# TensorE given products that nobody reads, in its waits of the prologue, the first chunk, the dt steps, the last sums and the first norm

## What is computed

```python
A = -jnp.exp(A_log)
xp = jnp.einsum('bld,rd->blr', x, x_proj_w)          # dt_in (16), B (16), C (16)
dt = softplus(jnp.einsum('blr,dr->bld', dt_in, dt_proj_w) + dt_proj_b)
dA = jnp.exp(dt[..., None] * A)
dBx = dt[..., None] * B[:, :, None, :] * x[..., None]
# h = dA_t * h + dBx_t along the 1024 tokens; y = sum over n of h * C_t, plus D * x
x = _layernorm(x + mixer(x))
x = _layernorm(x + silu_ffn(x))                      # 512 -> 1792 -> 512, float16 weights
x = _layernorm(x + attention(x))                     # 32 heads of 16, causal
x = _layernorm(x + int4_ffn(x))                      # 512 -> 1376 -> 512
```

## Time and profile before

| what | value |
|---|---|
| median of 3 runs | 903.16 us |
| the three runs | 903.12, 903.16, 908.68 us |
| the profiled execution | 909.25 us |
| its span, first to last instruction | 907.5 us |
| mean granted clock of PE | 0.955 |
| busy in the span: PE, DVE, ACT, POOL | 825.7, 647.1, 439.0, 308.9 us |

### The profile page before, as it was taken

One profiled execution on the slowest core, in us unless ns is written; L12 is line 12 of the kernel. 1 busy time (PEld: TensorE's weight loads), 2 busy tenths in 40 slices (PEclk: granted clock), 3 DMA queues, 4 the chain that ended last, 5 costly groups with the idle time before them and its releaser, 6 DMA issues.

```text
span 907.5 us, 19543 instructions
## 1 busy us (share of the span) xinstructions
PE 825.7 (91%) x8137; PEld 386.2 (43%) x8137; DVE 647.1 (71%) x912; ACT 439.0 (48%) x578; POOL 308.9 (34%) x219
## 2 busy tenths in 40 slices
PE   8758787786999999999979999999987999999997
PEld 2434343444544445455533444334423444444443
DVE  4998989995565334445567999999956978876334
ACT  4975646645754311244434666767676243333100
POOL 0798989993001010254420222121223222231000
PEclk8597979998999999999977999999998999999999
DMA  7800000004230000000000000000022113330011
GB/s 227 332 2 3 3 2 3 3 4 162 93 111 1 1 1 0 1 1 1 1 1 1 2 2 3 2 1 2 2 60 112 57 44 126 113 113 0 0 47 46
DMA packets 21937, 38.25 MB, mean 42 GB/s; under 512 B 6993, under 2 KB 12881, under 8 KB 21858
## 3 DMA queue, kind: packets, MB, share of 16 engines
q1 hardware_dynamic: 21858, 37.11, 11.9%
HBM read 34.87 MB, written 2.16 MB: 41 GB/s over the span
## 4 chain that ended last, share of the span: by engine, by line
PE 70%; DVE 17%; issue 6%; POOL 3%; ACT 2%; SPq 1%; DMA 1%; POOLq 0%; DVEq 0%; ACTq 0%
PE ps L864 13%; PE ps L664 11%; PE ps L641 8%; PE ps L891 6%; DVE arena L1543 6%; PE ps L815 6%; PE ps L715 5%; PE ps L751 5%; DVE arena L1344 4%; POOL arena L1196 3%; PE ps L799 3%; PE ps L514 3%; PE ps L558 2%; PE ps L728 2%; PE ps L755 2%
## 5 line engine op out<-in xcount | busy, mean ns | idle before, releaser
L1543 DVE TENSOR_REDUCE arena<-ps 128x1 f32<-128x512 f32 (+3 forms) x320 | 183.7, 630 | 20.8 <-PE ps L755 14.7
L1134 ACT ACTIVATE arena<-ps 128x1024 f32<-128x1024 f32 (+2 forms) x160 | 144.1, 941 | 77.9 <-PE ps L799 77.7
L1196 POOL TENSOR_TENSOR arena<-arena 128x1024 f32<-128x1024 f32 x64 | 159.7, 2524 | 14.3 <-DVE arena L1344 9.2
L1344 DVE TENSOR_TENSOR_SCAN arena<-arena,ps 128x1024 f32<-128x1024 f32 x64 | 142.6, 2272 | 9.8 <-ACT arena L979 6.0
L864 PE MATMUL ps<-arena 128*128 128x512 f16 x528 | 114.3, 379 | 1.6 <-DVE arena L1433 1.6
L1245 POOL TENSOR_SCALAR_AFFINE_SELECT arena<-arena 128x512 f32<-128x512 f32 x64 | 42.5, 664 | 185.6 <-ACT arena L1134 185.6
L664 PE MATMUL ps<-arena 128*128 128x512 f16 x448 | 97.5, 379 | 1.5 <-DVE arena L1474 1.5
L751 PE MATMUL ps<-arena 64*128 64x512 f16 (+3 forms) x384 | 97.6, 343 | 0.7 <-DVE arena L1543 0.7
L558 PE MATMUL ps<-arena 64*128 64x64 f16 x3072 | 61.5, 197 | 36.5 <-DVE arena L1344 32.7
L979 ACT ACTIVATE arena<-arena,negA 128x1024 f32<-128x1024 f32 x64 | 73.1, 1147 | 43.8 <-DVE arena L1344 42.8
L558 PEld LDWEIGHTS ps<-arena 64*128 64x128 f16 x3072 | 53.6, 100 | 90.4 <-DVE arena L1344 74.6
(11 more groups left out here) (155 smaller groups left out, 982.8 us busy)
## 6 DMA issues: line engine op xcount, KB each, us to landing
arena<-in_w_q_dram SPq DMA_DIRECT2D x11, 768.0 KB, 4.4
arena<-c_rows SPq DMA_DIRECT2D x16, 512.0 KB, 11.0
arena<-in_w_s_dram SPq DMA_DIRECT2D x11, 384.0 KB, 4.5
arena<-in_x_fm_dram SPq DMA_DIRECT2D x8, 256.0 KB, 4.0
out_dram<-arena SPq DMA_DIRECT2D x8, 256.0 KB, 2.0
arena<-in_wg_dram SPq DMA_DIRECT2D x1, 1792.0 KB, 9.7
arena<-in_wu_dram SPq DMA_DIRECT2D x1, 1792.0 KB, 7.3
arena<-in_wd_dram SPq DMA_DIRECT2D x1, 1792.0 KB, 11.3
```

The source lines that it names most:

```text
L1134: nc.scalar.activation(dst, src, ACT.Exp, scale=float(HD) ** -0.5).then_inc(exp_done, 1)
L1196: nc.gpsimd.tensor_tensor(hC[i % 4][:], hst[i % 3][:], c_all[:, n, :], ALU.mult).then_inc(hc_done, 1)
L1344: nc.vector.tensor_tensor_scan(hst[i % 3][:], dA[i % 3][:], banks(2 * (i % 2), 2), 0.0, ALU.mult, ALU.add).then_inc(scan_done, 1)
L1543: nc.vector.reduce_max(maxima_slot(half, k), ps[:, ring_bank(n), 0:len(heads) * w].rearrange("p (a w) -> p a w", a=len(heads)), AX).then_i ...
```

## The change

PE gets 153 more matmuls, each 128 rows by 128 columns of weights and 512 moving columns in float16. They write to bank 5 or bank 7 while nothing there is needed, and nobody reads them. 20 of them multiply the tile of zeros `warm`, the other 133 the gate weights `wg0_sb`, for which PE waits once on `ld_w0` between the two halves of `turn_dtx(0)`. In chunks 1 and 2 PE also waits for `z_pos` of the next chunk before they run, so that bank 5 is free. No other engine's program changes, apart from line numbers.

```diff
+            def idle_products(n, bank, tile=None, cols=HALF):
+
+                for _ in range(n):
+                    if tile is None:
+                        nc.tensor.matmul(banks(bank, 1), warm[:, 0:P], warm[:], start=True, stop=True)
+                    else:
+                        nc.tensor.matmul(banks(bank, 1), tile[:, 0:P], tile[:, 0:cols], start=True, stop=True)
...
-            x_linear(0, range(DC)).then_inc(xp_done, 1)
-            x_linear(1, range(DC // 2))
+            for c in range(DC - 1):
+                x_linear(0, (c,))
+                idle_products(2, 5)
+            x_linear(0, (DC - 1,)).then_inc(xp_done, 1)
+            idle_products(3, 5)
+            for c in range(DC // 2):
+                x_linear(1, (c,))
+                idle_products(2, 5)
             pe.wait_ge(ld_small, 4 * 16)
             dt_first(0)
-            x_linear(1, range(DC // 2, DC)).then_inc(xp_done, 1)
+            x_linear(1, (DC // 2,))
+            idle_products(2, 5)
+            x_linear(1, (DC - 1,)).then_inc(xp_done, 1)
+            idle_products(2, 5)
...
             dt_linear(1)
+            idle_products(3, 5)
             turn_dtx(0, range(TT // 2))
+            pe.wait_ge(ld_w0, 16)
+            idle_products(10, 5, wg0_sb[:, 0, :])
             turn_dtx(0, range(TT // 2, TT))
...
+                    if c == 0:
+                        idle_products({0: 2, 1: 10, 2: 10, 3: 5, 4: 5, 12: 0, 13: 0, 14: 0, 15: 0}.get(n, 4), 5, wg0_sb[:, 0, :])
+                    elif c + 1 < DC and 8 <= n < 11:
+                        pe.wait_ge(z_pos, c + 1)
+                        idle_products(5, 5, wg0_sb[:, 0, :])
             for n in range(NS - LAG, NS):
                 add_y((DC - 1) * NS + n)
+                idle_products(4, 5, wg0_sb[:, 0, :])
...
             for t in range(4):
                 turn_first(t)
+            idle_products(10, 7, wg0_sb[:, 0, :])
             turn_normed(0)
+            idle_products(3, 7, wg0_sb[:, 0, :])
             turn_normed(1)
             turn_first(4)
             turn_normed(2)
             turn_first(5)
             turn_normed(3)
+            idle_products(4, 7, wg0_sb[:, 0, :])
```

## The result

The changed kernel took 908.57 us (median of 22 runs, 903.35 to 914.67). The kernel before, beside it on the same chip, took 904.14 us (22 runs, 899.96 to 910.72). The ratio is 1.0048, with a 95% interval of 1.0031 to 1.0065: 4.4 us slower, a small loss, and well inside the 1% that the prediction called no change. Further down, the ratios of y1 and y3 leave out one disturbed run each (1060.17 and 977.9 us), which their medians keep.

What follows compares the result with a forecast made beforehand. DVE was taken to set the pace in the long low-clock stretch, PE in the prologue and at the beginnings of chunks 1 and 2. 2.6 + 0 + 0 + 0 + 0 - 0.7 = +1.9 us gave 905.0 us, range 899.5 to 910.0.

Steps and rivals of the forecast that it cites:

- main case: Whole kernel: forecast 905.0 us, bracket 902.5 to 907.5, chance 0.50.
- rival B: Around 20 us and early chunk 0: low clock meets the products, slower; 907.8 us, up to 910; chance 0.18.
- Input products: Prologue: fifteen products ahead of the last input product delay `xp_done` and DVE's copy; +2.6 us.
- Turns: Prologue, around the two turns: -0.35 us at full clock, +1 to +2 at low clock; entered as 0.
- Chunk 0: Chunk 0: 60 products hidden by DVE with the clock up, cost 0; low clock up to 2 us per ten.
- Beginnings of chunks: Starts of chunks 1 and 2: no reason for the falls to go; 0 against the median, ends -4.4 and +4.4.
- Dt steps: Chunks 1 and 2: thirty products fit PE's waits; 0, or a gain of 1 to 2 where the clock falls.
- Last sums and norm: Last four sums and first norm: products keep the clock up, turns run faster; -0.7 us, between 0 and -1.5.
- A: Beginnings of chunks 1 and 2: all falls go, clock stays up; 902.5 us, perhaps 900; chance 0.22.
- C: Whole kernel: products, 20 of them on zeros, do not hold the clock, only costs remain; 909.4 us; chance 0.05.
- D: All 51 us of low clock were lost time and half comes off; 886 us; chance 0.02.

Runs made afterwards that it cites:

- y1: Changed kernel without its products ahead of chunk 0 (123 left), PE's wait for `ld_w0` moved behind the turns: 904.37 us, ratio 0.9985.
- y3: Changed kernel without the products of the prologue, the last sums and the norm (90 left, in the chunks): 905.19 us, ratio 1.0005.
- x2: Kernel before with only the 17 products between and behind the input products: 908.57 us, ratio 1.0042.
- x1: Changed kernel without the 17 products between and behind the input products, other 136 kept: 904.39 us, ratio 1.0008.
- x3: Changed kernel with the 15 products between the input products put in one block ahead of the last input product: 909.03 us, ratio 1.0044.
- z4: Changed kernel run again, unchanged, for a second trace: 908.88 us, ratio 1.0040.
- x4: Kernel before run again, unchanged, for a second trace: 903.17 us, ratio 0.9986.
- y4: y1 plus four products behind the last step of chunks 0 to 2 and three in step 0 of chunks 1 and 2: 903.95 us, ratio 0.9982.
- z1: y4 without the three products of step 0; four behind the last step of chunks 0 to 2 stay: 903.91 us, ratio 0.9996.
- z2: z1 with POOL's step 6 product in chunks 1 and 2 waiting until DVE's first dt instruction ends: 900.32 us, ratio 0.9961.
- y2: Kernel before with only the 33 products behind the last four sums and in the first norm: 904.35 us, ratio 0.9991.
- z3: Kernel before with only the POOL wait of z2: 903.22 us, ratio 0.9995.

## Why the prediction was right, and where a term was off

The forecast was 905.0 us, against a median of 903.16 for the kernel before; the change measured +4.4 us, the forecast says +1.9. Direction, place of the loss and the verdict within 1% were right, and 908.57 is inside the range, near its upper end. It is not inside the 902.5 to 907.5 of the main case, which had a chance of 0.50; it lies in the bracket of rival B (907.5 to 910), whose condition the profile after does not meet. About 1 us of the distance is the baseline, 904.14 in the comparison and 903.16 in the forecast. That the range holds the number owes something to luck: some 2 of the 4.4 us are in no term of the sum (see what stays open). Point by point:

**Input products, +2.6 us: right in mechanism, too small.** The copy went from 14.70 to 19.10 in the pair of profiles. Over all traces it starts at 15.2 on average in the ten without these products (14.70 to 15.79) and at 18.5 in the three that interleave them (18.20, 18.31, 19.10), where 17.3 was forecast: 3.4 us. The first scan moves by about 3.0, to 29.75 and 30.56 in the two traces of the changed kernel, where 28.9 was forecast. The term of the sum that was mis-sized is the price of one product: "0.21 us each" was read from sixteen of one shape in a row, and between float32 products it is 0.34. Six groups (the one ahead of `dt_first` makes no new change of shape for an input product) at 0.14 for the slower pair behind them, six pairs of products at 0.54 and one three at 0.76 are 4.8 us; less PE's waits for the second half of x in the profile before, 0.28 us ahead of 9.70 and 0.11 ahead of 10.70 (the lower end of the prediction's 0.4 to 0.8), 4.4. In the other nine traces without these products the first of the two waits alone is 0.6 to 1.8 us, and in the three with them there is none; the products fill that wait, and so the mean over the traces is 3.4 and not 4.4. x2 shows that this term stands alone for the loss, x1 that without it there is none to be measured, x3 that in a block the price is 0.23.

**Turns, taken as 0 between -0.35 and +1 to +2: both ends occur.** With the clock up (after) the wait of DVE before the first scan shrank from 0.59 to 0.30 us. With the clock low (x1) the first scan came at 28.07; the other nine without input products have it at 27.1 on average, so the ten products cost 1 us there. In the changed kernel the input products themselves come ahead of this place, and in its two traces the clock was up for the ten (after) or fell for 3.4 us (z4). In both it is 11.45 us from DVE's copy to the first scan, against 11.9 in the kernel before: the gain of 0.35 came, as about 0.45.

**Chunk 0, 0: right.** It lasts 48.9 or 49.0 us in 13 of the 14 traces, with the 60 products and without them, at the full clock and with 15 us of low clock in it (49.3 in x4, where the clock fell at 64.9). DVE hides PE there in both directions.

**Beginnings of chunks, taken as 0 against the median with 4.4 us either way: right that the change does not steer them, wrong in their worth.** Over the 14 traces a fall stands at the first beginning in 6 and at the second in 5. Of the kernel before, one trace has the first and the other has not; of the changed kernel, one has the second and the other has not. The traces of the three kernels with products in step 15 (y4, z1, z2) have none at either; six places of six, against 11 falls in 22 places elsewhere, which speaks for these products but rests on one trace each. The price of the first was read from DVE's waits, 1.35 + 3.02. Those are there, but in six of the eight traces without them chunk 1 lasts 45.6 to 45.9 us, not 42.5 (46.9 less 4.4): DVE's dt instruction then takes 4.9 to 5.6 us and not 2.4, and gives back up to 3.2 of the 4.4. A fall there is then worth 1.2 us. The other two are x4, where that instruction took 2.84 us and chunk 1 42.9, and z2. The second is worth the 4.5 us by which chunk 2 differs (46.9 and 42.4), a little above the 3.6 that the waits sum to.

**Dt steps, 0: no cost is seen, but the products do not hold the clock.** It did fall there in seven of the 14 traces (102.5 after, 100.9 in z4), with five products in each of the three steps or, in y2, without them. In the profile after it fell inside PE's longest idle time of the chunk, the 4.12 us ahead of 103.10, in which PE waited for the scan behind the long dt instruction:

```profile
103.10 1.46 PE L575 MATMUL ps<-arena 64*128 64x64 f16 x48 [4.12 <-DVE arena L1373]
```

The traces divide by that instruction. In the six in which it took 4.9 to 5.6 us, PE then sat idle for 3.4 to 5.3 us and the clock fell within it, at 98.0 to 102.5 us; z2, with 3.32 us and an idle time of 1.8, has a fall too, at 98.7. In the seven in which it took 2.4 to 2.8 us, PE's longest idle time there was 2.5 us and the clock stayed up.

**Last sums and norm, -0.7: right, somewhat small.** -0.9 to -1.4 by the traces. The turns took 1.94 us, where 1.8 was forecast:

```profile
210.01 1.94 PE L658 MATMUL ps<-ident_sb,arena 128*128 128x128 f32 x16 [0.65 <-DVE arena L1379]
210.67 0.70 DVE L1487 BATCH_NORM_STATS2 st<-ps 128x6 f32<-128x512 f32 x1 [0.81 <-PE ps L658]
```

**The rivals.** A: both falls were gone in the profile after, and one of them stayed in z4, so it is not something that the change does each time. B: its mechanism is in x1's trace, for 1.1 us of the 2.7 that it adds up. C: falls for the kernel as a whole; in the profile after the low clock is 3.4 us of the first 221. The 17 products alone (x2: low from 21.1 us for 23.9) and the other 136 alone (x1: from 18.4 for 6.8) do not hold the clock at the turns; together they did in after and x3, and in z4 all but 3.4 us. The argument against C, that the input products ran fast behind products on zeros, holds only from 6.7 us on; the first input product was slow still. D: 48 us of low clock went in the pair of profiles and the median rose by 4.4. By the rule that the Trainium skill's page "TensorE: Matmul & The Clock Gate" (section Terms) gives, those 48 us would be worth half, 24 us, an estimate. The traces agree with it at the beginning of chunk 2 only, where 10.2 us of low clock cost 4.5; at that of chunk 1 they cost 1.2 in the end, and in chunk 0, where DVE is the fuller engine, 14 to 15 us cost nothing.

**What stays open.** The traces give the change about +3.0 at the first scan and -0.9 to -1.4 at the norm, some 2 us; the medians say 4.4 and 5.3 us (z4), and 3.9 for x2 alone. The other 2 us are not explained, but the traces show where they may lie. The part behind the norm, the same instructions in every kernel, lasts 684.5, 686.9, 686.2 and 687.0 us in the four traces with the input products (x2, x3, after, z4) and 683.6 on average in the ten without (681.3 to 686.1), with 35 and 30 us of low clock in it. That is 2.5 us, the size that is missing. Four traces against ten with this spread can be chance, and why products of the first 20 us should lower the clock hundreds of us later no run shows. The forecast took this part as not touched.

## What to carry to other kernels

A low clock of PE is a loss only where PE is what the others wait for: read the busy time of the other engines in the same stretch before filling PE's gaps. Here DVE was 97% busy and more in the two long stretches from 17 to 75 us, and the higher clock gave nothing there. Products put between operations of another shape on the path cost more than the same ones in a row (here 0.34 us against 0.23), and a chain that ran without a gap pays every one of them. A chain that waits for a DMA in some executions hides part of them, so one trace misprices them. When a stall goes away in one execution, look further down the same stage for what became longer; and look at a second profile of the unchanged kernel before giving a change the credit for what moved.

## What the hardware showed that was not expected

**DVE's dt instruction is held by POOL.** It reads two SBUF tiles of 128 x 1024 in float32; it takes 1.20 us in chunk 0 and 2.4, 2.8, 3.3, 4.9 or 5.6 us in chunk 1, and in all 14 traces it ends there 1.1 us after the end of a POOL product that also reads SBUF. In the changed kernel:

```profile
95.10 5.62 DVE L1355 SCALAR_TENSOR_TENSOR arena<-arena 128x1024 f32<-128x1024 f32 x1
```
```profile
85.64 14.01 POOL L1225 TENSOR_TENSOR arena<-arena 128x1024 f32<-128x1024 f32 x6
```

The Trainium skill's page "SBUF — State Buffer" (section "SBUF: two separate sides") says that such a DVE operation and a GpSimd operation exclude each other for a whole instruction, and that the one that started first goes on. The traces agree with that for one product of POOL. They show more: the instruction started at 95.10, POOL's product in work then ended at 97.33, the next one ran from 97.26 to 99.64 (the ends on POOL are rough), and only behind that did DVE's end, at 100.72. It missed one change from product to product. z2, in which POOL did not offer the next product, brought it to 3.32 us. Why it missed the change in z1 and after, and took it before (2.38), is not settled. What the traces have is the time since POOL's product began: 0.13 to 0.17 us in the five of 5.6 us, 0.9 in y4 (4.9 us), 0.6 in x4 (2.84 us, one product waited for), 1.1 in the six of 2.4 us.

**One fall, two prices.** Because of this, a fall of the clock that delays DVE by 4.4 us at the beginning of chunk 1 has cost only 1.2 us by its end. Taking it away alone (z1) or letting DVE go first alone (z3) gives nothing measurable; both together (z2) gave 3.3 us.

**Places of the falls.** In one kernel the clock fell at 75.0 us in one execution, at the end of chunk 0, and at 64.9 in another, some 10 us ahead of it; the fall at the beginning of chunk 2 (122.8 and 119.5) came in both. The low stretches in the chunks lasted 3.4, 6.8 or 10.2 us.
